# Expert stage of a four-layer kernel: products of two stages reordered and reshaped on one core

## The chip, the cores and the metric

One core of a Trainium2 chip runs the whole kernel. The metric is the device time of one execution in microseconds (us), given as the median of several runs.

## The reference

2,048 rows of 128 numbers pass four layers: a banded attention, a mixture of experts whose experts are Kronecker products, a state-space mixer with a short convolution, and a soft mixture of experts. Only the second one, cut here, is touched:

```python
def kmoe(x_flat, W_router, A, B, scale, bias, d_in1, d_in2, d_out1, d_out2, top_k):
    logits = x_flat @ W_router.T
    vals, idx = jax.lax.top_k(logits, top_k)
    probs = jax.nn.softmax(vals, axis=-1)
    xs = x_flat.reshape(-1, d_in1, d_in2)
    Y = jnp.einsum('nkoi,nij,nkpj->nkop', A[idx], xs, B[idx])
    out = jnp.einsum('nkop,nk->nop', Y, probs).reshape(-1, d_out1 * d_out2)
    return out * scale + bias
h = gelu(kmoe(x.reshape(-1, 1024), up ..., 32, 32, 64, 64, 2))
y = kmoe(h, down ..., 64, 64, 32, 32, 2)
```

There are 256 tokens of 32x32 numbers and 64 experts, of which two are taken for a token. Each of the two calls forms, for a token and an expert, A x B^T as two small products.

## The kernel before

All of this is in `kmoe` (line 648). The five engines run instruction lists of their own, written out by hand, and meet at semaphores: `wait_ge` holds back all that stands behind it on its engine. The order of the work is the order of those lists. An fp32 product appears in the trace as two matmul records with a weight load each, a transpose as one. Blocks end with a barrier of all engines, after which the next layer starts.

**Up stage.** The 256 tokens are taken in `NB` = 4 blocks `j`. `first` (L988, matmul L993) multiplies four tokens at a time, laid out block by block in `x4`, by the B tables of both experts, 16 groups `f` of four products, into banks 6 and 7 in turn. ScalarE copies each bank to `z` (`take_z`, L895, L900). `second` (L996, matmul L1007) multiplies `z` by the A tables, 128 products for a block, 32 rows by 64 columns, in two pairs, adding the two experts in PSUM. VectorE applies scale and bias (L815) into `h`, and ScalarE the gelu, two activations for a block (`gelu`, L902, L906), once the block's four parts are there. TensorE's order is first(0), first(1), second(0), first(2), second(1), first(3), second(2), second(3). ScalarE's is take_z(0), then take_z(j+1), gelu(j). The next stage (L1025) waits for all gelus. In parallel SP loads the tables of the down experts (L738 to L741), once the last up table has been gathered.

**Down stage.** The tokens are taken in `NCH` = 8 chunks. `first_down` (L1060, L1067) makes 32 products of 64 by 64 into two banks (4, 5 or 6, 7), which ScalarE copies to `vs`, one after the other (`take_v`, L922, L927). `second_down` (L1071, L1082) makes 64 products with 64 rows and 32 columns, expert by expert, adding the experts in PSUM banks 0 and 1. Chunks 2gr and 2gr+1 fill different partitions. After both, VectorE takes them out with scale and bias (`take_y`, L828, L833) into `yb`, TensorE turns them by four transposes (`rows_out`, L1086, L1093) into a bank of natural rows, and the layer norm follows: statistics and factors on VectorE (L75, L84 to L102), the root on ScalarE (L112), scaled rows on ScalarE (L933), the sum on GpSimd or VectorE (L749, L849). VectorE's list is take_y(0), then norm_y(gr), take_y(gr+1); ScalarE's is take_v(0) to take_v(5), norm_y(0), take_v(6), take_v(7), norm_y(1) to norm_y(3). TensorE's:

```python
for ch in range(NCH):
    second_down(ch)
    if ch + 2 < NCH:
        first_down(ch + 2)
    if ch >= 2 and ch % 2 == 0:
        rows_out(ch // 2 - 1)
rows_out(3)
```

The rows below also hold lines from elsewhere in this layer and the next: L958 (router logits, whose weights are read every 64 bytes of a row) and L950 (transposes of contiguous columns). L1031, L1214 and L826 are a 64-column product with a full load, a 512-column product, and a copy of one bank by VectorE.

Of the kernel before, what the change touches and what calls it, by code (L numbers as in the profile page):

```python
# [11 lines left out]
ALU = mybir.AluOpType  # L12
# [3 lines left out]
P = 128  # L16
# [631 lines left out]
def kmoe(nc, x, c, d):  # L648
# [5 lines left out]
    with ExitStack() as ctx:  # L654
# [11 lines left out]
        bias_dn = a.sb("bias_down", [P, D1])  # L666
# [14 lines left out]
        yb = a.sb("y_block", [P, 2, 8, 2, D1])  # L681
# [14 lines left out]
        y_rows = x4[:, 0:NT, :]  # L696
        oht_up = oht[:, :, :, :].rearrange("p a k (m g) -> p a k m g", m=2)
# [12 lines left out]
        v_done, v_ready, y_done, y_ready, nat_done, y_added = (a.sem(k) for k in ("v_psum", "v_ready", "y_psum", "y_ready", "y_rows_psum", "y_added"))  # L710
# [13 lines left out]
        with nc.Block() as block:  # L724
# [27 lines left out]
            def _(dve):  # L752
# [75 lines left out]
                def take_y(gr):  # L828
                    dve.wait_ge(y_done, 2 * gr + 2)
                    if gr >= 2:  # L830
                        dve.wait_ge(nat_done, gr - 1)
                    for w in range(2):
                        v.scalar_tensor_tensor(out=yb[:, gr % 2, :, w, :], in0=psum[:, w, 0:8 * D1].rearrange("p (n a) -> p n a", n=8), scalar=scales[:, 1:2],  # L833
                                               in1=bias_dn[:, :].unsqueeze(1).broadcast_to([P, 8, D1]), op0=ALU.mult, op1=ALU.add).then_inc(y_ready, 1)

                def norm_y(gr):
                    dve.wait_ge(nat_done, gr + 1)
                    for t in range(4):
                        ln_y.tile_stats(4 * gr + t, psum[:, nat_bank(gr), P * t:P * t + P])
                    ln_y.finish(dve, 4 * gr, 4 * gr + 4, gr)  # L840

                take_y(0)
                for gr in range(4):
                    norm_y(gr)
                    if gr < 3:
                        take_y(gr + 1)
# [5 lines left out]
            def _(act):  # L852
# [42 lines left out]
                def take_z(j):  # L895
                    if j >= 2:
                        act.wait_ge(h_done, 2 * j - 2)
                    for f in range(4 * j, 4 * j + 4):
                        act.wait_ge(z_done, f + 1)
                        s.copy(z[:, j % 2, 4 * (f % 4):4 * (f % 4) + 4, :, :].rearrange("p g k n -> p (g k n)"), psum[:, 6 + f % 2, :]).then_inc(z_ready, 1)  # L900

                def gelu(j):  # L902
                    act.wait_ge(hb_ready, 4 * j + 4)
                    for k in range(2):
                        part = h[:, 32 * j + 16 * k:32 * j + 16 * k + 16, :].rearrange("p n o -> p (n o)")
                        s.activation(part, part, ACT.Gelu).then_inc(gelu_done, 1)  # L906

                take_z(0)
                for j in range(NB):
                    if j + 1 < NB:  # L910
                        take_z(j + 1)
                    gelu(j)
# [9 lines left out]
                def take_v(ch):  # L922
# [3 lines left out]
                    for k in range(2):  # L926
                        s.copy(vs[:, ch % 4, k, :, :, :].rearrange("p n k b -> p (n k b)"), psum[:, v_bank(ch) + k, :]).then_inc(v_ready, 1)  # L927

                def norm_y(gr):
                    ln_y.root(act, 4 * gr, 4 * gr + 4, gr)  # L930
# [5 lines left out]
                for ch in range(6):  # L936
                    take_v(ch)
                norm_y(0)
                take_v(6)
                take_v(7)  # L940
                for gr in range(1, 4):
                    norm_y(gr)
# [976 lines left out]
```

## Time and profile before

| what | value |
|---|---|
| median of 3 runs | 874.09 us (869.92 to 874.47) |
| the profiled execution's own time | 870.78 us |
| its span | 868.8 us |
| TensorE busy | 654.9 us (75%), 7,522 matmul records |
| VectorE, ScalarE, GpSimd busy | 519.9, 344.7, 358.8 us |
| up stage | 342.0 to 390.8 us |
| down stage | 434.6 to 487.3 us |

The span is what the profiler sees between the first and last instruction; the execution's own time holds some 2 us more. In the rows below PE is TensorE's matmuls, PEld its weight loads, DVE is VectorE, ACT is ScalarE and POOL is GpSimd. "PEclk" in a window is the granted TensorE clock as a share of 2.4 GHz: 0.50 is 1.2 GHz. The time in brackets at the end of a row is how long the engine stood idle before it, and what ended that; "issue" means that nothing in the profile did.

### The profile page before, as it was taken

To read this page: it belongs to the slowest core of one execution; us is meant where nothing else is said; L and a number is where in the kernel's file an instruction comes from. 1 tells how busy PE (TensorE), PEld (TensorE's weight loads), DVE (VectorE), ACT (ScalarE), POOL (GpSimd) and SP (SyncE) were. 2 spreads that over 40 slices of the span, in tenths; PEclk is the share of its full clock that TensorE was granted. 3 is DMA by queue.
4 is the path that set the end of the run, shared out by engine and by line. 5 is a ranking of instruction groups with operands and counts; after the bars stand their busy time and mean duration, and the time that the engine had idled before them with its cause. 6 is when DMAs were issued, how large, how long until landed. Compare 5 with 4: busy or idle time off the path is not lost. (4 is left out here: it accounts for less than half of the span.)

```text
span 868.8 us, 18294 instructions
## 1 busy us (share of the span) xinstructions
PE 654.9 (75%) x7522; PEld 386.0 (44%) x7554; DVE 519.9 (60%) x1094; ACT 344.7 (40%) x522; POOL 358.8 (41%) x330
## 2 busy tenths in 40 slices
PE   0627878788786389868875478248998988999995
PEld 0313444444444389758765324123333344444442
DVE  8656666676664633221502668878999984415265
ACT  1422444334443653330423463246554535434320
POOL 9202444444442300000001062328998983966530
PEclk9968999999998579878868599659999998999999
DMA  3156540000000632200000470000000000000000
GB/s 76 36 120 150 68 66 0 0 0 0 0 1 1 223 85 49 53 3 2 2 5 5 136 235 0 0 0 1 0 1 0 0 1 1 1 0 1 12 13 24
DMA packets 17326, 29.75 MB, mean 34 GB/s; under 512 B 3248, under 2 KB 13168, under 8 KB 16240
## 3 DMA queue, kind: packets, MB, share of 16 engines
q1 hardware_dynamic: 17264, 28.87, 13.1%
q8 instruction: 46, 0.75, 0.3%
q14 instruction: 16, 0.13, 0.1%
HBM read 24.54 MB, written 4.19 MB: 33 GB/s over the span
## 5 line engine op out<-in xcount | busy, mean ns | idle before, releaser
L474 ACT ACTIVATE pr_exp<-at_psum 128x1024 f32<-128x1024 f32 x68 | 69.6, 1024 | 128.2 <-PE at_psum L559 128.2
L366 DVE TENSOR_REDUCE pr_neg_max<-at_psum 128x4 f32<-128x1024 f32 x68 | 83.2, 1225 | 49.7 <-PE at_psum L541 49.7
L316 POOL TENSOR_SCALAR_AFFINE_SELECT pr_exp<-pr_exp 128x512 f32<-128x512 f32 x68 | 47.1, 692 | 155.6 <-ACT pr_exp L474 155.6
L1481 POOL TENSOR_TENSOR all_phi_b<-all_phi_b,mo_work 128x512 f32<-128x512 f32 x56 | 71.0, 1268 | 44.6 <-ACT mo_work L1687 40.0
L749 POOL TENSOR_TENSOR all_x<-all_x,ff_x_blocks 128x512 f32<-128x512 f32 x3 | 3.8, 1267 | 187.5 <-ACT ff_x_blocks L933 187.5
L1502 PE MATMUL all_psum<-all_phi,mo_xt 128*128 128x512 f32 x128 | 66.3, 645 | 7.4 <-ACT mo_work L1669 5.6
L1451 POOL TENSOR_TENSOR mo_work<-mo_work,mo_max 128x1024 f32<-128x1024 f32 x32 | 61.4, 1918 | 21.5 <-DVE mo_max L1743 21.5
L536 PE MATMUL at_psum<-band_mask,all_ident_bf 128*128 128x512 bf16 x104 | 35.7, 401 | 40.9 <-DVE pr_q_window L359 27.6
L1535 PE MATMUL all_psum<-mo_xt,all_phi_centred 128*128 128x512 f32 x128 | 66.3, 598 | 0.0
L1588 PE MATMUL all_psum<-mo_work,mo_y_slots 128*128 128x512 f32 x128 | 62.5, 595 | 1.8 <-DVE mo_work L1791 1.8
L1687 ACT ACTIVATE mo_work<-all_psum 128x512 f32<-128x512 f32 x64 | 37.7, 601 | 61.9 <-PE all_psum L1535 61.9
L1457 POOL TENSOR_TENSOR mo_dispatch<-mo_work,mo_rsum 128x1024 f32<-128x1024 f32 x32 | 61.4, 1920 | 0.0
L1511 PE MATMUL all_psum<-mo_dispatch,mo_xn 128*128 128x512 f32 x128 | 60.1, 593 | 0.0
L1673 ACT ACTIVATE mo_work<-mo_work 128x1024 f32<-128x1024 f32 x32 | 33.9, 1059 | 55.5 <-POOL mo_work L1451 55.5
L553 PE MATMUL at_psum<-pr_neg_max_t,band_select 128*128 128x256 bf16 x272 | 41.6, 276 | 5.9 <-ACT pr_exp L474 5.5
L1791 DVE TENSOR_TENSOR mo_work<-mo_work,all_psum 128x512 f32<-128x512 f32 x64 | 38.9, 681 | 11.9 <-PE all_psum L1577 11.9
L318 POOL TENSOR_SCALAR_AFFINE_SELECT pr_exp<-pr_exp 128x512 f32<-128x512 f32 x68 | 45.8, 673 | 0.0
L1502 PEld LDWEIGHTS all_psum<-all_phi,mo_xt 128*128 128x128 f32 x128 | 23.5, 201 | 47.0 <-ACT mo_work L1669 24.8
L573 PE MATMUL at_psum<-pr_exp,pr_v_window 128*32 128x128 f32 x1088 | 41.7, 278 | 1.4 <-POOL pr_exp L318 1.4
L1743 DVE TENSOR_REDUCE mo_max<-mo_work 128x32 f32<-128x1024 f32 x32 | 38.7, 1209 | 6.5 <-ACT mo_work L1669 6.5
L1750 DVE TENSOR_REDUCE mo_sum<-mo_work 128x32 f32<-128x1024 f32 x32 | 38.7, 1209 | 0.0
L1511 PEld LDWEIGHTS all_psum<-mo_dispatch,mo_xn 128*128 128x128 f32 x128 | 24.3, 191 | 30.7 <-issue 29.6
(339 smaller groups left out, 1335.6 us busy)
## 6 DMA issues: line engine op xcount, KB each, us to landing
all_expert_w<-in_expert_w SPq DMA_DIRECT2D x1, 4096.0 KB, 18.2
ff_b_up<-in_b_up SPq DMA_DIRECT2D x1, 2048.0 KB, 9.1
ff_a_up<-in_a_up SPq DMA_DIRECT2D x1, 2048.0 KB, 14.0
ff_w_down<-in_w_down SPq DMA_DIRECT2D x2, 1024.0 KB, 20.7
at_q_stack<-parts_scratch SPq DMA_DIRECT2D x24, 64.0 KB
at_k_stack<-parts_scratch SPq DMA_DIRECT2D x24, 64.0 KB
at_q_stack<-parts_scratch SPq DMA_DIRECT2D x12, 128.0 KB
at_k_stack<-parts_scratch SPq DMA_DIRECT2D x12, 128.0 KB
```

Source lines behind the costliest of these rows:

```text
L316: nc.gpsimd.affine_select(out=e[:, g, :, 0, :], in_=e[:, g, :, 0, :], compare_op=ALU.is_ge, fill=0.0, base=0, pattern=[[0, GH], [-1, P]], ...
L318: nc.gpsimd.affine_select(out=e[:, g, :, 1, :], in_=e[:, g, :, 1, :], compare_op=ALU.is_ge, fill=0.0, base=0, pattern=[[0, GH], [1, P]], c ...
L366: nc.vector.tensor_reduce(negm[:, GH * g:GH * g + GH].rearrange("p (u r) -> p r u", r=2), psum[:, SN + 2 * (g % 2):SN + 2 * (g % 2) + 2, : ...
L474: nc.scalar.activation(e[:, g, :, :, :].rearrange("p h j q -> p (h j q)"), psum[:, ST:ST + 2, :].rearrange("p b n -> p (b n)"), ACT.Exp).t ...
L573: last = nc.tensor.matmul(psum[32 * k:32 * k + 32, PV, P * g:P * g + P], vw[:, sp, j, h, :], e[:, g, k, j, :], start=(j == 0), stop=(j == 1))
L1451: nc.gpsimd.tensor_tensor(cells(ls[:, u % 4, :]), cells(lc[:, u % 4, :]), to_cells(mn[:, u % 4, :]), ALU.subtract).then_inc(sub_done, 1)
L1457: nc.gpsimd.tensor_tensor(cells(dn[:, u % 4, :]), cells(ls[:, u % 4, :]), to_cells(rs[:, u % 4, :]), ALU.mult).then_inc(d_ready, 1)
L1481: nc.gpsimd.tensor_tensor(tot[:, ch % 2, :], first, ec[:, ch % 2, j, :], ALU.add).then_inc(added, 1)
L1502: last = nc.tensor.matmul(psum[:, 2 * hf + k, :], xt[:, P * z:P * z + P], phi_d[:, HALF * hf + W * k:HALF * hf + W * k + W], start=True, s ...
L1511: last = nc.tensor.matmul(psum[:, 4 + 2 * hf + k, :], xn[:, z, :], dn[:, u % 4, W * k:W * k + W], start=(z == 0), stop=(z == NT - 1))
L1535: nc.tensor.matmul(psum[:, n % 3, :], phi[:, P * j:P * j + P], xt[:, cols], start=False, stop=True).then_inc(cl_done, 1)
L1588: nc.tensor.matmul(psum[:, 5 + ch % 2, :], yt[:, j, :], ec[:, ch % 2, j, :], start=(j == 0), stop=(j == NJ - 1)).then_inc(y_done, 1)
```

## The change

- **Up stage, order on TensorE.** `first` now makes one group `f` and `second` a quarter of a block (one pair, half of the groups). After first(0) to first(3) each quarter of block j is followed by one group of block j+1; the last block's quarters follow each other. ScalarE's list copies two groups and then applies one gelu of a pair (one activation with 1,024 elements, strided rows), from the second pair on. The waits on banks are given by pair.
- **Down stage, shape.** `second_down` makes 32 products for a chunk instead of 64: both experts' 64 columns of `vs` by both experts' 64 columns of A. The two 32x32 blocks of the same expert in each 64x64 result are wanted, the two mixed ones are not used. Each chunk fills all of banks 0 and 1, and is taken out at once with the scale: bank 0 by ScalarE, bank 1 by VectorE.
- **Down stage, rows.** `rows_out` runs for every chunk instead of every second. Instead of a transpose it makes 8 products with 64 of the identity's columns (`pick`), which select the rows of one expert, turn them and add both in the natural bank. The bias comes first, as a product of an 8-row selector (`row_of`, a new copy on VectorE ahead of the xt copies) by the bias as 8 rows of 128.
- **Down stage, who copies.** The first of the two `vs` banks is copied by ScalarE, the second by VectorE, and the parts of the layer norm are spread in both lists. `yb` lies in a free part of `x4`.

Added lines (removed ones only where they are short; the rest of them are in the listing above):

```diff
@@ -663,7 +663,7 @@
...
-        bias_dn = a.sb("bias_down", [P, D1])
+        bias_dn = a.sb("bias_down", [R, P])
...
@@ -678,7 +678,7 @@
...
-        yb = a.sb("y_block", [P, 2, 8, 2, D1])
+        row_of = a.sb("row_of", [R, P])
...
@@ -694,6 +694,7 @@
...
+        yb = x4[:, NT:2 * NT, :].rearrange("p g n -> p (g n)").rearrange("p (u k n w a) -> p u k n w a", u=2, k=K, n=8, w=2)
...
@@ -797,6 +798,7 @@
...
+                v.tensor_copy(row_of[:, :].rearrange("r (n q) -> r n q", q=R), c["ident"][0:R, 0:R].unsqueeze(1).broadcast_to([R, 16, R])).then_inc(halves_ready, 1)
...
@@ -825,25 +827,37 @@
...
+                def take_v(ch):
+                    dve.wait_ge(v_done, ch + 1)
+                    if ch >= 4:
+                        dve.wait_ge(y_done, ch - 3)
+                    v.tensor_copy(vs[:, ch % 4, 1, :, :, :].rearrange("p n k b -> p (n k b)"), psum[:, v_bank(ch) + 1, :]).then_inc(v_dve, 1)
+
+                def take_y(ch):
+                    dve.wait_ge(y_done, ch + 1)
+                    if ch >= 2:
+                        dve.wait_ge(nat_done, ch - 1)
+                    v.tensor_scalar(yb[:, ch % 2, :, :, 1, :], psum[:, 1, :].rearrange("p (n k a) -> p k n a", n=8, k=K), scales[:, 1:2], None, ALU.mult).then_inc(y_dve, 1)
...
+                    dve.wait_ge(nat_done, 2 * gr + 2)
...
+                    ln_y.variance(dve, 4 * gr, 4 * gr + 4)
+
+                take_v(0)
+                take_v(1)
+                for ch in range(NCH):
+                    take_y(ch)
+                    if ch + 2 < NCH:
+                        take_v(ch + 2)
+                    if ch >= 3 and ch % 2 == 1:
+                        norm_y(ch // 2 - 1)
+                    if ch >= 4 and ch % 2 == 0:
+                        ln_y.invert(dve, 2 * ch - 8, 2 * ch - 4, ch // 2 - 2)
+                ln_y.invert(dve, 8, 12, 2)
+                norm_y(3)
+                ln_y.invert(dve, 12, NT, 3)
...
@@ -892,24 +906,27 @@
...
+                def take_z(f):
+                    j = f // 4
...
+                    act.wait_ge(z_done, f + 1)
+                    s.copy(z[:, j % 2, 4 * (f % 4):4 * (f % 4) + 4, :, :].rearrange("p g k n -> p (g k n)"), psum[:, 6 + f % 2, :]).then_inc(z_ready, 1)
+
+                def gelu(n):
+                    act.wait_ge(hb_ready, 2 * n + 2)
+                    rows = h[:, 32 * (n // 2):32 * (n // 2) + 32, :].rearrange("p (g r) o -> p g r o", r=4)[:, :, 2 * (n % 2):2 * (n % 2) + 2, :]
+                    s.activation(rows, rows, ACT.Gelu).then_inc(gelu_done, 1)
+
+                for f in range(4):
+                    take_z(f)
+                for n in range(2 * NB):
+                    if n < 2 * NB - 2:
+                        take_z(2 * n + 4)
+                        take_z(2 * n + 5)
+                    if n >= 1:
+                        gelu(n - 1)
+                gelu(2 * NB - 1)
...
@@ -923,23 +940,33 @@
...
+                    s.copy(vs[:, ch % 4, 0, :, :, :].rearrange("p n k b -> p (n k b)"), psum[:, v_bank(ch), :]).then_inc(v_act, 1)
+
+                def take_y(ch):
+                    act.wait_ge(y_done, ch + 1)
+                    if ch >= 2:
+                        act.wait_ge(nat_done, ch - 1)
+                    s.activation(yb[:, ch % 2, :, :, 0, :], psum[:, 0, :].rearrange("p (n k a) -> p k n a", n=8, k=K), ACT.Copy, scale=scales[:, 1:2]).then_inc(y_act, 1)
...
+                take_v(0)
+                take_v(1)
+                for ch in range(NCH):
+                    take_y(ch)
+                    if ch + 2 < NCH:
+                        take_v(ch + 2)
+                    if ch >= 3 and ch % 2 == 1:
+                        ln_y.root(act, 2 * ch - 6, 2 * ch - 2, ch // 2 - 1)
+                    if ch >= 4 and ch % 2 == 0:
+                        norm_y(ch // 2 - 2)
+                norm_y(2)
+                ln_y.root(act, 12, NT, 3)
+                norm_y(3)
...
@@ -984,38 +1011,41 @@
...
+                def first(f):
+                    if f >= 2:
+                        pe.wait_ge(z_ready, f - 1)
+                    for k in range(4):
+                        g = 4 * f + k
+                        last = t_.matmul(psum[:, 6 + f % 2, P * k:P * k + P], x4[:, g, :], gb_up[:, g, :, :].rearrange("p k n -> p (k n)"), start=True, stop=True)
+                    last.then_inc(z_done, 1)
+
+                def second(j, pair, part):
+                    q = 4 * j + 2 * pair
+                    if part == 0:
+                        pe.wait_ge(z_ready, 4 * j + 4)
+                        if q >= 6:
+                            pe.wait_ge(hb_ready, q - 4)
+                    for g2 in range(4 * part, 4 * part + 4):
+                        for k in range(K):
+                            for s in range(2):
+                                for r in (2 * pair, 2 * pair + 1):
+                                    rows = slice(32 * r, 32 * r + 32)
+                                    last = t_.matmul(psum[64 * s:64 * s + 64, h_bank(4 * j + r), F1 * g2:F1 * g2 + F1], z[rows, j % 2, 2 * g2 + s, k, :],
+                                                     ga_up[rows, 16 * j + 2 * g2 + s, k, :], start=(k == 0), stop=(k == K - 1))
+                    if part == 1:
...
+                for f in range(4):
+                    first(f)
...
+                    for pair in range(2):
+                        for part in range(2):
+                            second(j, pair, part)
+                            if j + 1 < NB:
+                                first(4 * j + 4 + 2 * pair + part)
...
@@ -1024,7 +1054,7 @@
...
-                pe.wait_ge(halves_ready, 1)
+                pe.wait_ge(halves_ready, 2)
...
@@ -1059,7 +1089,8 @@
...
+                        pe.wait_ge(v_act, ch - 1)
+                        pe.wait_ge(v_dve, ch - 1)
...
@@ -1069,28 +1100,35 @@
...
+                    pe.wait_ge(v_act, ch + 1)
+                    pe.wait_ge(v_dve, ch + 1)
+                    if ch >= 1:
+                        pe.wait_ge(y_act, ch)
+                        pe.wait_ge(y_dve, ch)
...
+                            for tl in range(2):
+                                for w in range(2):
+                                    rows, n2 = slice(64 * w, 64 * w + 64), 4 * tl + nn
+                                    last = t_.matmul(psum[64 * tl:64 * tl + 64, w, 64 * idx:64 * idx + 64], vs[rows, ch % 4, s, n2, :, :].rearrange("p k b -> p (k b)"),
+                                                     ga_dn[rows, 64 * s + 8 * ch + n2, :, :].rearrange("p k a -> p (k a)"), start=True, stop=True)
...
+                def rows_out(ch):
+                    gr = ch // 2
...
+                    pick = c["ident"][:, :].rearrange("p (c k b) -> p k c b", c=2, k=K)
+                    if ch % 2 == 0:
+                        if gr >= 2:
+                            pe.wait_ge(ln_y.by_act, 4 * (gr - 1))
+                        t_.matmul(psum[:, nat_bank(gr), :].rearrange("p (c n) -> p c n", c=4), row_of[:, :], bias_dn[:, :].unsqueeze(1).broadcast_to([R, 4, P]), start=True, stop=False)
+                    pe.wait_ge(y_act, ch + 1)
+                    pe.wait_ge(y_dve, ch + 1)
+                    for k in range(K):
+                        src = yb[:, ch % 2, k].rearrange("p n w (r q) -> p q (n w r)", q=4)
+                        for q in range(4):
+                            last = t_.matmul(out[:, q, 2 * (ch % 2):2 * (ch % 2) + 2, :], src[:, q], pick[:, k], start=False, stop=(ch % 2 == 1 and k == K - 1 and q == 3))
...
@@ -1101,9 +1139,9 @@
...
-                    if ch >= 2 and ch % 2 == 0:
-                        rows_out(ch // 2 - 1)
-                rows_out(3)
+                    if ch >= 1:
+                        rows_out(ch - 1)
+                rows_out(NCH - 1)
...
@@ -1889,7 +1927,7 @@
...
-        "bias_down": np.tile(moe["bias_down"].reshape(32, 32).T, (4, 1)),
+        "bias_down": moe["bias_down"].reshape(8, 128),
...
```

## Rows read from the trace of the kernel before

**Rows 1.** windows: us, busy (records) of PE, PEld, DVE, ACT, POOL; PEclk, DMA share, GB/s
```profile
342.00:391.00 49.00, 36.50 (x1158) 34.47 (x1160) 11.97 (x17) 18.23 (x25) 0.00 (x0) 0.83 0.20 46
442.50:455.50 13.00, 10.41 (x434) 9.15 (x432) 0.88 (x2) 3.13 (x6) 0.00 (x0) 0.50 0.02 5
434.60:487.30 52.70, 31.05 (x1552) 27.34 (x1552) 12.60 (x64) 16.61 (x37) 3.80 (x3) 0.70 0.02 4
```

**Rows 2.** timeline of TensorE, down stage: start us, us, what, [idle before <-releaser]
```profile
434.70 1.51 PE L1067 MATMUL ff_psum<-ff_b_taken,ff_h 64*64 64x64 f32 x88 [0.89 <-DVE ff_a_taken L826]
437.99 0.81 PE L1067 MATMUL ff_psum<-ff_b_taken,ff_h 64*64 64x64 f32 x40 [1.77 <-issue]
438.73 0.96 PE L1082 MATMUL ff_psum<-ff_a_taken,ff_b_up 64*32 64x32 f32 x88
441.44 0.56 PE L1082 MATMUL ff_psum<-ff_a_taken,ff_b_up 64*32 64x32 f32 x40 [1.75 <-issue]
441.93 1.67 PE L1067 MATMUL ff_psum<-ff_b_taken,ff_h 64*64 64x64 f32 x64
443.52 0.54 PE L1082 MATMUL ff_psum<-ff_a_taken,ff_b_up 64*32 64x32 f32 x24
444.89 1.61 PE L1082 MATMUL ff_psum<-ff_a_taken,ff_b_up 64*32 64x32 f32 x104 [0.83 <-issue]
...
465.70 1.98 PE L1067 MATMUL ff_psum<-ff_b_taken,ff_h 64*64 64x64 f32 x64
...
481.60 1.13 PE L1093 MATMUL ff_psum<-all_ident,ff_y_block 128*128 128x128 f32 x4 [0.99 <-DVE ff_y_block L833]
```

**Rows 3.** DMA queues, 434 to 487 us: packets, MB, share of 16 engines
```profile
q8 instruction: 13, 0.21, 1.6%
```

**Rows 4.** waits, 434 to 487 us: who waited for whom, us, times, longest
```profile
DVE ff_ln_y_tmp L100 <- ACT ff_ln_y_tmp L112: 9.3, 4, 5.2
PE ff_psum L1082 <- DVE ff_y_block L833: 6.6, 2, 4.0
```

**Rows 5.** timeline of TensorE, up stage
```profile
342.02 7.61 PE L993 MATMUL ff_psum<-ff_b_taken,ff_x_blocks 128*128 128x128 f32 x64
...
355.23 2.61 PE L1007 MATMUL ff_psum<-ff_a_taken,ff_b_up 32*64 32x64 f32 x85 [3.04 <-issue]
...
363.84 4.18 PE L1007 MATMUL ff_psum<-ff_a_taken,ff_b_up 32*64 32x64 f32 x256
...
378.87 2.06 PE L1007 MATMUL ff_psum<-ff_a_taken,ff_b_up 32*64 32x64 f32 x127 [1.29 <-issue]
382.53 3.43 PE L1007 MATMUL ff_psum<-ff_a_taken,ff_b_up 32*64 32x64 f32 x128 [1.60 <-issue]
386.26 0.92 PE L1007 MATMUL ff_psum<-ff_a_taken,ff_b_up 32*64 32x64 f32 x23 [0.30 <-issue]
```

**Rows 6.** timeline of ScalarE, up stage
```profile
345.94 0.59 ACT L900 COPY ff_b_up<-ff_psum 128x512 f32<-128x512 f32 x1 [0.31 <-PE ff_psum L993]
...
388.68 2.00 ACT L906 ACTIVATE ff_h<-ff_h 128x1024 f32<-128x1024 f32 x2 [5.73 <-DVE ff_h L815]
```

**Rows 7.** timeline and lines: prices (durations in ns as min/median/max, first and last start)
```profile
409.96 0.63 PE L1031 MATMUL ff_psum<-ff_half_sum,ff_logits_t 128*128 128x64 f32 x4 [0.48 <-DVE ff_logits_t L819]
...
357.77 3.31 PE L993 MATMUL ff_psum<-ff_b_taken,ff_x_blocks 128*128 128x128 f32 x16
...
L958 PEld LDWEIGHTS ff_psum<-ff_w_up,ff_h x32: 291/310/313, 300.2 to 306.9; 128*128 128x128 f32 x32
...
L1093 PEld LDWEIGHTS ff_psum<-all_ident,ff_y_block x16: 196/224/226, 454.4 to 482.1; 128*128 128x128 f32 x16
...
L950 PEld LDWEIGHTS ff_psum<-all_ident,ff_h x16: 183/226/231, 295.0 to 298.9; 128*128 128x128 f32 x16
...
L1214 PE MATMUL all_psum<-all_phi,sm_centre x8: 592/592/697, 542.3 to 545.4; 128*128 128x512 f32 x8
...
L826 DVE COPY ff_b_taken<-ff_psum x8: 691/692/692, 417.1 to 424.7; 128x512 f32<-128x512 f32 x8
```

More of the change, by code:

```diff
@@ L985, in _ @@
                     take_up(u)
-                def first(j):
-                    for f in range(4 * j, 4 * j + 4):
-                        if f >= 2:
-                            pe.wait_ge(z_ready, f - 1)
-                        for k in range(4):
-                            g = 4 * f + k
-                            last = t_.matmul(psum[:, 6 + f % 2, P * k:P * k + P], x4[:, g, :], gb_up[:, g, :, :].rearrange("p k n -> p (k n)"), start=True, stop=True)
-                        last.then_inc(z_done, 1)
@@ L996, in second @@
-                def second(j):
-                    pe.wait_ge(z_ready, 4 * j + 4)
-                    for r in range(4):
-                        if 4 * j + r >= 6:
-                            pe.wait_ge(hb_ready, 4 * j + r - 5)
-                    for pair in ((0, 1), (2, 3)):
-                        for g2 in range(8):
-                            for k in range(K):
-                                for s in range(2):
-                                    for r in pair:
-                                        rows = slice(32 * r, 32 * r + 32)
-                                        last = t_.matmul(psum[64 * s:64 * s + 64, h_bank(4 * j + r), F1 * g2:F1 * g2 + F1], z[rows, j % 2, 2 * g2 + s, k, :],
-                                                         ga_up[rows, 16 * j + 2 * g2 + s, k, :], start=(k == 0), stop=(k == K - 1))
+                def first(f):
[5 more added lines that the diff above has]
+                    last.then_inc(z_done, 1)
@@ L1009, in second @@
                         last.then_inc(h_done, 1)
                 pe.wait_ge(x4_part, 16)
-                first(0)
+                for f in range(4):
+                    first(f)
                 pe.wait_ge(took_act, UB)
@@ L1015, in _ @@
                 for j in range(NB):
-                    if j + 1 < NB:
-                        first(j + 1)
-                    second(j)
+                    for pair in range(2):
[3 more added lines that the diff above has]
+                                first(4 * j + 4 + 2 * pair + part)
                 pe.wait_ge(wdn_loaded, 32)
@@ L1077, in second_down @@
                             idx = 4 * (nn // 2) + 2 * s + nn % 2
-                            for k in range(K):
-                                for tl in range(2):
-                                    for w in range(2):
-                                        rows, col, n2 = slice(64 * w, 64 * w + 64), 32 * (2 * (ch % 2) + tl), 4 * tl + nn
-                                        last = t_.matmul(psum[col:col + 32, w, D1 * idx:D1 * idx + D1], vs[rows, ch % 4, s, n2, k, :],
-                                                         ga_dn[rows, 64 * s + 8 * ch + n2, k, :], start=(k == 0), stop=(k == K - 1))
+                            for tl in range(2):
[3 more added lines that the diff above has]
+                                                     ga_dn[rows, 64 * s + 8 * ch + n2, :, :].rearrange("p k a -> p (k a)"), start=True, stop=True)
```

51 lines of the change are left out of this document (1 added, 50 removed).

## The prediction

> **What bounds the kernel now.** I read the profile by stages, since the change touches two stages only. In the windows [rows 1] the up products take 342.0 to about 390.8 us with TensorE busy 36.5 of 49 us, and the down products 434.6 to 487.3 us with TensorE busy 31.1 of 52.7 us. No other engine is near full there (VectorE 12.6, ScalarE 16.6 us), so what counts is why TensorE stands still.
>
> In the timeline of the down stage [rows 2] much of the idle time is put down to "issue", nothing that the profile shows. It is regular. TensorE resumes at 437.99, 441.44 and 444.89 us, 3.45 us apart each time, and between two resumptions it runs 40+88 = 128 and then 40+64+24 = 128 matmul records. Each has its weight load, so 256 instructions. The instruction queue moved 13 packets of 16 KB in this stage [rows 3], one for about 240 of its 3,104 matmul and load instructions. I read this as instruction fetch: a block of 128 matmul records costs TensorE the larger of its work and 3.45 us. The stage's 1,552 records [rows 1] are 12.1 blocks, a floor of 41.8 us, under the 47.9 us from its first matmul to the end of its last at 482.7 us [rows 2]. The rest is waits: 6.6 us for the y evacuation L833, which stood behind the layer norm on VectorE, itself behind ScalarE's root (L100 waited 9.3 us for L112) [rows 4].
>
> The Trainium skill says otherwise (Runtime: NRT & Kernel Launch, "Instruction fetch mechanics"): crossing a 16 KiB block is mostly hidden, because the sequencer issues more slowly than the fetch fills. The blocks agree with the trace, the hiding doesn't: three resumptions come after 0.83 to 1.77 us of idle time [rows 2]. What its rule would give is a rival below.
>
> The up stage shows the same: resumptions at 382.53 and 386.26 us with 128 records between, and a longer hole of 3.04 us before 355.23 us [rows 5], when the down tables were landing (SP issues them once the last up table is gathered, near 342 us; the DMA share of this stage is 0.20, that of the down stage 0.02 [rows 1]).
>
> **The up stage.** Nothing is removed: 128 records of first and 1,024 of second. A quarter of second (64 records) costs 4.18/4 = 1.0 us and four products of first (8 records) 7.61/8 = 0.95 us, at the full clock [rows 5]. Now eight such products stand in a row and each waits for a copy out of one of two banks; after the change they lie between quarters, and the copies (0.59 us [rows 6]) lie beside second. ScalarE's gelu pair (2.00 us [rows 6]) no longer stands before the copies of the next block. New is a wait: the quarter that opens a block needs the copy of the product just before it, which I put at 0.8 us, 0.59 and a hand-over on either side.
>
> - Start: 342.0, four firsts to 345.8, wait to 346.6 us.
> - Blocks 0 to 2: 4 x 1.95 + 0.8 = 8.6 us each, above their fetch floor (288 records, 7.8 us), 25.8 us.
> - Block 3: 256 records with nothing between, two fetches, 6.9 us; the same stretch now takes 386.26 - 378.87 = 7.4 us. I take 7.2.
> - The fetch under the table loads: the records up to the hole are the same in number, but are used up earlier, at about 351.1 us. Normal supply would bring the next block right then (stall 0); the old arrival would be 355.2 us (stall 4.1). The old request waited some 1.8 us longer than usual, so I take 1.8.
>
> The sum is 346.6 + 25.8 + 7.2 + 1.8 = 381.4 us against an end of 387.2 us now: 5.8 us. The end gains more: the next stage waits for the last gelu, now two activations in 2.00 us, then one, 1.0 us less. I take 6.5 us for the stage, a little off for half clock after the stall. Bounds: 3 (stall 4.1, half clock after it) to 8.5 (no stall). VectorE's work (L815) is unchanged. Its banks' waits are not stricter.
>
> **The down stage.** Second falls from 1,024 records of 32 columns to 512 of 64 columns: the same column work, half the instructions. They have the shape of first_down: 88 records in 1.51 us, which less one pipeline length is 15 ns each [rows 2]; at half clock (the 64 records in 1.98 us) 27 ns. Now 128 records cost about 1.5 us, then 64 cost 1.0: no gain where TensorE works, only in fetch. The 16 transposes (one record each) become 64 pick products of two records: 128 records with a full 128-column load. The four records of L1031 have that load and 64 columns: 0.63 us, or 112 ns each after the first [rows 7]. At half clock the nearest is L993, 16 in 3.31 us, 207 ns [rows 7]. The bias is 4 products of 8 rows by 512 columns, 8 records, priced by L1214 at (545.4-542.3)/7 = 0.44 us [rows 7]. All in all 1,160 records, 9.1 blocks, a floor of 31.3 us.
>
> Per chunk at full clock: 1.0 + 1.0 + 16 x 0.112 + 0.44 = 4.2 us. Its 145 records have a fetch floor of 3.9 us, so TensorE becomes the bound, by a little. Step by step:
>
> - The first 128 records are first_down(0) and (1), unchanged: the resumption stays at 437.99 us.
> - The next block is 40 of first, 64 of second, 24 of first: 1.9 us of work, then 441.44 us as now.
> - The next ends with a stall to about 444.9 us. The clock of this stretch is half from 442.5 on [rows 1], as now. To the end of the first picks it then takes 1.1 (first) + 1.7 (bias) + 3.4 (picks), to about 451 us at half clock, about 450 if it rises on the way.
> - Left are 6 seconds (6.0), 4 firsts (4.0), 7 sets of picks (12.6), 3 biases (2.6): 25.2 us of full-clock work for 758 records, whose floor is 20.4 us. With 1.0 us for blocks that lie badly: 476.2 us.
>
> Now the last record ends at 482.7 us, so the stage gains 6.5 us. The waits that could stand in its way: y of a chunk is copied (0.69 us on VectorE, like L826 [rows 7], 0.59 us on ScalarE) while TensorE does first(ch+2) and picks(ch-1), 2.8 us. VectorE's norm now begins after the copies of its chunk and waits for the root a chunk later, so L833's wait is gone. Per two chunks VectorE has 4 x 0.69 plus a norm of about 2 us, under the 8.4 us of TensorE. The added v copy on VectorE spares ScalarE one of two. The y copies read twice the columns, but lie on two engines. The work after the last product stays. Bounds: gain 9.5 (full clock from the start of the stage) to a loss of 15 (below).
>
> **Small edits.** The row selector copy on VectorE stands before the xt copies: under 0.3 us. Bias rows and more wait instructions: some 0.3 us of fetch that the 1.0 covers. No DMA is added, and SP and POOL keep their order.
>
> **Sum.** -6.5 - 6.5 + 0.3 = -12.7 us against the profiled execution's 870.78 us: 858.1 us. The median of the runs, 874.09 us, lies 3.3 us above that execution, the lowest, 869.92 us, below it. I predict 860.0 us.
>
> **Rivals.**
> - *Half clock in the down stage (slower).* The picks are the dearest records at half clock. A chunk then costs 1.7 + 1.7 + 3.4 + 0.85 = 7.7 us, eight of them 61 us, an end near 498 us: 15 us lost, 6.5 gained above, 879 us. It decides in the down stage: each us at half clock does 0.55 us of work, so after the 7 us that I assume, some 28 us more at 1.2 GHz take the gain away. For it: the stage has a mean of 0.70 now [rows 1]. Against: it is idle 40% of the time now, which goes. 0.06.
> - *Strided weights (same).* The pick weights are read every 16 bytes. L958, read every 64 bytes, takes 310 ns a load and (306.9-300.2)/31 = 216 ns a record [rows 7]. If the picks did, they would cost 128 x 0.104 = 13.3 us more: 871.4 us. Against: L1093's loads, every 16 bytes, take 224 ns as L950's contiguous ones do (226) [rows 7]. 0.09. The Trainium skill (SBUF, State Buffer, "Door 1: The DMA port swizzle") has lines of 16 bytes and asks for two hits on each for full speed, which speaks for the rival; in the same note it lets four fp32 go free, which speaks for mine.
> - *The holes are not fetch (slower).* If "issue" idle time stays whatever the count, the down stage swaps work of 18 us (512 records x 15 ns, 1,024 x 8.7 by the 88 in 0.96 us, 16 x 0.11 us [rows 2]) for 33 us (8 x 4.2), less 7.6 us of waits on L833: 7.5 us longer, with 2 us won above: 876 us. That is what the Runtime page's rule would do here. The 3.45 us period speaks against it. 0.04.
> - *The tables hold the fetch (a smaller gain).* The up stage gains 3 us: 861.6 us, inside my forecast.
>
> **How the numbers follow.** My forecast has 0.78; 0.03 is for what I have not seen, 0.02 of it faster and 0.01 the same. This measurement tells about 0.5% (4.4 us) from no change: faster means under 869.7 us. Faster 0.78 + 0.02 = 0.80, same 0.09 + 0.01 = 0.10, slower 0.06 + 0.04 = 0.10. Low is 852 us (8.5 + 9.5 gained, 853, and a low run), high 871 us, which takes in the weak forms of the rivals.
>
> **What would show it.** After the change the down stage has 1,160 matmul records, picks 112 ns apart, "issue" holes only in its first 10 us, no wait for a y copy over 1 us, a clock above 0.85, and a last matmul some 34 to 42 us after its first. In the up stage no wait for z above 1 us and a stage of 41 to 46 us from its first matmul to the first of L1025's kind. Wrong would be: picks 200 ns apart at the full clock, holes that keep their sum, or a half clock past 460 us.

## The result and the profile after

The changed kernel takes 908.69 us (906.69 to 909.88, four runs) where the kernel before takes 873.13 us (869.92 to 874.47, four runs): a ratio of 1.041, 95% interval 1.038 to 1.045. It is 36 us slower; the forecast was 860.0 us in a range that ended at 871 us. The profiled execution's span is 907.2 us, against 868.8 us. Of all executions in this document two, both of `late_packed` below (873.42 and 876.38 us), lie over 1.5% above the fastest of their kernel; the ratios leave them out.

The stages, from the first matmul of the up stage to the first of the router logits, and in the down stage from its first matmul to the start of the last transpose or pick:

| kernel, profiled execution | up stage | down stage | rest of the span |
|---|---|---|---|
| before | 48.8 us | 47.6 us | 772.4 us |
| changed | 62.3 us | 66.0 us | 778.9 us |
| forecast | about 42 us | 41.5 us | unchanged |

The edits cost 13.5 and 18.4 us. 4.3 us of the rest lie before the up stage, which begins at 346.3 instead of 342.0 us. I don't charge them to the change: of the kernels below, which share that code, one begins it at 341.7 and another at 346.4 us.

These are the windows of the changed kernel, split where the clock falls; the columns are those of [rows 1]:

```profile
346.20:360.80 14.60, 10.48 (x250) 9.66 (x247) 2.10 (x3) 3.52 (x6) 0.00 (x0) 1.00 0.65 145
360.80:408.50 47.70, 42.89 (x908) 39.18 (x906) 9.86 (x14) 15.08 (x19) 0.00 (x0) 0.50 0.01 3
452.80:518.90 66.10, 61.18 (x1160) 55.42 (x1160) 17.12 (x55) 16.61 (x32) 3.80 (x3) 0.68 0.01 3
```

TensorE is hardly idle any more: it is busy 61.2 of 66.1 us in the down stage (31.1 of 52.7 in [rows 1]) and 42.9 of 47.7 us in most of the up stage. The 1,160 records are those of the forecast. The work itself has become dearer. In the up stage one row says why, the granted clock: 0.50, that is 1.2 GHz, for 47.7 us on end. Its timeline (L1033 is second, L1019 first, L1055 the logits):

```profile
353.11 1.16 PE L1033 MATMUL ff_psum<-ff_a_taken,ff_b_up 32*64 32x64 f32 x64
354.20 1.16 PE L1019 MATMUL ff_psum<-ff_b_taken,ff_x_blocks 128*128 128x128 f32 x8
355.29 1.14 PE L1033 MATMUL ff_psum<-ff_a_taken,ff_b_up 32*64 32x64 f32 x59
359.79 0.33 PE L1033 MATMUL ff_psum<-ff_a_taken,ff_b_up 32*64 32x64 f32 x5 [3.36 <-issue]
...
371.94 2.08 PE L1019 MATMUL ff_psum<-ff_b_taken,ff_x_blocks 128*128 128x128 f32 x8
373.94 1.99 PE L1033 MATMUL ff_psum<-ff_a_taken,ff_b_up 32*64 32x64 f32 x64
...
399.06 6.76 PE L1033 MATMUL ff_psum<-ff_a_taken,ff_b_up 32*64 32x64 f32 x256 [0.73 <-ACT ff_b_up L914]
408.53 18.69 PE L1055 MATMUL ff_psum<-ff_h,ff_w_down 64*64 64x128 f32 x256 [2.71 <-ACT ff_h L919]
```

At first a quarter and a group start 1.09 us apart (1.0 and 0.95 us were costed). After one hole of 3.4 us under the table loads they start 2 us apart, and the clock does not rise again before the stage is over. In the kernel before, the clock fell too (half from 353.6 to 360.4 us), but its 16 records of first in a row [rows 7] ran just there, and it was full from 360.4 to 380.9 us:

```profile
353.60:360.40 6.80, 5.17 (x97) 5.05 (x97) 1.41 (x2) 1.07 (x2) 0.00 (x0) 0.50 0.01 2
360.40:380.90 20.50, 16.59 (x671) 15.32 (x670) 5.63 (x8) 7.19 (x11) 0.00 (x0) 1.00 0.02 4
```

The down stage (L1098 is first_down, L1114 second_down, L1125 the bias, L1131 the picks), and the load of the picks:

```profile
452.86 1.51 PE L1098 MATMUL ff_psum<-ff_b_taken,ff_h 64*64 64x64 f32 x88 [0.89 <-DVE ff_a_taken L828]
456.15 0.81 PE L1098 MATMUL ff_psum<-ff_b_taken,ff_h 64*64 64x64 f32 x40 [1.77 <-issue]
456.78 1.11 PE L1114 MATMUL ff_psum<-ff_a_taken,ff_b_up 64*64 64x64 f32 x64
457.71 0.52 PE L1098 MATMUL ff_psum<-ff_b_taken,ff_h 64*64 64x64 f32 x23
459.59 0.85 PE L1098 MATMUL ff_psum<-ff_b_taken,ff_h 64*64 64x64 f32 x41 [1.36 <-issue]
460.23 1.15 PE L1114 MATMUL ff_psum<-ff_a_taken,ff_b_up 64*64 64x64 f32 x64
461.16 0.53 PE L1098 MATMUL ff_psum<-ff_b_taken,ff_h 64*64 64x64 f32 x21
463.42 0.91 PE L1098 MATMUL ff_psum<-ff_b_taken,ff_h 64*64 64x64 f32 x43 [1.73 <-issue]
464.26 1.12 PE L1125 MATMUL ff_psum<-ff_bias_down,ff_row_of 8*128 8x512 f32 x2
465.31 4.00 PE L1131 MATMUL ff_psum<-all_ident,ff_x_blocks 128*128 128x64 f32 x16
...
472.86 3.95 PE L1131 MATMUL ff_psum<-all_ident,ff_x_blocks 128*128 128x64 f32 x16
```
```profile
L1131 PEld LDWEIGHTS ff_psum<-all_ident,ff_x_blocks x128: 307/329/332, 465.3 to 518.8; 128*128 128x128 f32 x128
```

Two things are to be seen. The holes come as forecast, 3.44 and 3.83 us apart with 127 and 126 records between them, and the matmuls have none after 463.4 us, once picks lie in every block. And a set of picks takes 4.0 us instead of 1.8 or 3.4. Its records start 233 ns apart (median) at either clock, and a load takes 329 ns, like the 310 ns of L958 in [rows 7] and not like that of a contiguous one (192 ns, below). The set at 472.86 us ran almost wholly at the full clock, and the small products after it at half:

```profile
472.80:476.70 3.90, 3.90 (x24) 3.81 (x16) 0.69 (x1) 0.59 (x1) 0.00 (x0) 0.92 0.00 0
485.30:488.90 3.60, 3.60 (x129) 3.49 (x128) 0.75 (x1) 0.69 (x1) 0.00 (x0) 0.50 0.02 5
```

So the mean of 0.68 flatters the stage. From 469.2 us on the clock was full only while picks, which gain nothing from it, and a bias product ran; practically all the products of first and second ran at half.

### The profile page after: what moved, and what is told of

Read it like the earlier page. It is cut to its first block and busy times, and to the rows that moved or that the text cites. A ratio compares the mean times of both kernels' runs of the same rounds, so it can differ in the third digit from the quotient of the medians.

```text
span 907.2 us, 17592 instructions
## 1 busy us (share of the span) xinstructions
PE 712.0 (78%) x7162; PEld 431.4 (48%) x7162; DVE 527.8 (58%) x1103; ACT 347.1 (38%) x522; POOL 359.4 (40%) x330
## 5 line engine op out<-in xcount | busy, mean ns | idle before, releaser
L536 PE MATMUL at_psum<-band_mask,all_ident_bf 128*128 128x512 bf16 x136 | 43.1, 400 | 38.6 <-DVE pr_q_window L359 38.6
L1540 PE MATMUL all_psum<-all_phi,mo_xt 128*128 128x512 f32 x128 | 65.3, 636 | 7.2 <-ACT mo_work L1707 5.6
L553 PE MATMUL at_psum<-pr_neg_max_t,band_select 128*128 128x256 bf16 x272 | 41.6, 276 | 5.9 <-ACT pr_exp L474 5.5
L1540 PEld LDWEIGHTS all_psum<-all_phi,mo_xt 128*128 128x128 f32 x128 | 23.5, 198 | 44.9 <-issue 23.4
L817 DVE SCALAR_TENSOR_TENSOR ff_h<-ff_psum,ff_scales,ff_bias_up 128x512 f32<-128x512 f32 x16 | 11.3, 746 | 48.9 <-PE ff_psum L1033 48.9
```

The lines of the kernel that those rows point to most:

```text
L536: nc.tensor.matmul(psum[:, SN + 2 * (g % 2) + r, :], c["identb"][:, :], c["mask"][:, :, :].rearrange("p a b -> p (a b)"), start=True, stop ...
L1540: last = nc.tensor.matmul(psum[:, 2 * hf + k, :], xt[:, P * z:P * z + P], phi_d[:, HALF * hf + W * k:HALF * hf + W * k + W], start=True, s ...
```

## The experiments

The ratios compare each kernel with executions of the kernel before taken beside it: these have a median of 877.13 us for the first four kernels, 876.61 us for the next four (`late_packed` to `one_run`, on another chip) and 874.78 us for the last three.

**1. One edit at a time.** `down_only` is the changed kernel with the take_z, gelu, first and second code of before:

```diff
-                for j in range(NB):
-                    for pair in range(2):
-                        for part in range(2):
-                            second(j, pair, part)
-                            if j + 1 < NB:
-                                first(4 * j + 4 + 2 * pair + part)
+                for j in range(NB):
+                    if j + 1 < NB:
+                        first(j + 1)
+                    second(j)
```

> The new down stage with the old order of the up stage. Theory: the two edits lose independently; the up stage goes back to about 48.8 us from its first matmul to the first of the router logits (62.3 in the changed kernel), the down stage stays at about 71 us: 909 - 13.4 = 895 us. Rival: the up stage's loss comes from something that both edits share (place of the instructions, state of the clock before); then it stays above 55 us and the time above 902 us.

893.91 us (890.56 to 898.36), ratio 1.021 (1.017 to 1.026). The up stage is back at 48.8 us, the down stage takes 64.4 us at a clock of 0.72.

`up_only` is the reverse, the kernel before with that piece of the changed one.

> The new order of the up stage alone, with the down stage of before. Theory: the up stage takes about 62 us, with the granted clock at 0.5 from its first fetch hole to its end, and the rest is as before: 873 + 13.4 = 886.5 us. Rival: the reorder is harmless by itself (870 to 874 us).

891.35 us (887.69 to 894.27), ratio 1.016 (1.011 to 1.022). The up stage takes 63.2 us with the clock at half from 357.8 to 412.4 us, the down stage 48 us as before. So each edit loses alone, 17 and 14 us by the medians; the sum is 31 us, where both together cost 36.

**2. The pick weights.** `packed_picks` changes where the y copies put each number, so that the 128 weights of a pick are neighbours. Each copy is split in two for it:

```diff
-        yb = ....rearrange("p (u k n w a) -> p u k n w a", u=2, k=K, n=8, w=2)
+        yb = ....rearrange("p (u k q n w r) -> p u k q n w r", u=2, k=K, q=4, n=8, w=2)
...
-                        src = yb[:, ch % 2, k].rearrange("p n w (r q) -> p q (n w r)", q=4)
+                        src = yb[:, ch % 2, k].rearrange("p q n w r -> p q (n w r)")
```

> The changed kernel, with the y copies laid out so that the weights of each pick product are 128 contiguous numbers instead of every fourth one (each copy is split in two for it). Theory: the pick records took 244 ns because their weights are read every 16 bytes; contiguous they take 112 ns at the full clock or about 213 at half, so the stage gets 4 to 17 us shorter: 892 to 905 us. Rival: a load for a 64-column product that adds into a bank costs this anyway (or the bank's 32-column runs do): records stay at 244 ns, 909 us.

886.89 us (883.33 to 896.41), ratio to before 1.010 (1.005 to 1.016), where the changed kernel has 1.041. The profiled execution is the slowest of the four, so its stages are longer than those of the median. The picks of its trace, first across a rise of the clock (473.6 us), then at the full clock, last at half, and their loads:

```profile
472.61 2.44 PE L1135 MATMUL ff_psum<-all_ident,ff_x_blocks 128*128 128x64 f32 x16
...
478.05 2.00 PE L1135 MATMUL ff_psum<-all_ident,ff_x_blocks 128*128 128x64 f32 x16
...
499.80 7.09 PE L1135 MATMUL ff_psum<-all_ident,ff_x_blocks 128*128 128x64 f32 x32
```
```profile
L1135 PEld LDWEIGHTS ff_psum<-all_ident,ff_x_blocks x128: 186/270/338, 466.0 to 506.4; 128*128 128x128 f32 x128
```

A record now costs 112 ns at the full clock and 213 at half. Nothing about the product changed but the distance of its weights, so the cause of the 233 ns is shown, and the rival (the accumulation or the 32-column runs of the output) is out. The stage's first to last matmul went from 66.0 to 53.2 us.

**3. The hole under the table loads.** `late_tables` keeps the loads of the down tables back until the last up product:

```diff
                 sp.wait_ge(got, 2 * UB)
+                sp.wait_ge(h_done, 2 * NB)
```

> The changed kernel, with the loads of the down tables held back until the last product of the up stage, so that no load competes with the fetch of instructions there. Theory: the 3.4 us hole under the loads is what lets the clock fall, and the mix of quarters and groups then cannot raise it; without the hole the up stage runs at the full clock in 36 to 41 us: 884 to 889 us. Rival: the mix of small and large products lets the clock fall by itself; only the hole's 3.4 us go: about 905 us.

887.15 us (885.03 to 888.22), ratio 1.011 (1.007 to 1.016), the theory's figure. The up stage took 42.9 us, a little over the 36 to 41 expected, without a hole for 37 us and at the full clock for its first 38.9 us:

```profile
344.80:383.70 38.90, 34.06 (x1131) 31.14 (x1129) 10.56 (x15) 17.55 (x24) 0.00 (x0) 1.00 0.02 4
```

`before_late` has the same line in the kernel before:

> The kernel before with the late tables alone, the control. Theory: only the 3 us hole and the half clock behind it go, up stage 44 to 46 us, 873 to 875 us. If the late tables carry all of the gain of the kernel with the new order and late tables, this is 871 us or less, and the reorder is worth nothing.

876.12 us (870.01 to 879.01), ratio 0.998 (0.995 to 1.001): nothing. The up stage took 48.3 us, not the 44 to 46 that I expected: a hole of 1.5 us was left at the same place, the clock fell to half there all the same (358.8 to 365.6 us), and the waits for ScalarE were still there. The late loads also have a price: in every kernel that has them the time from the first router logits to the first matmul of the down stage is 45.3 to 46.9 us, where the others take 43.4 to 44.3.

**4. Both cures, and the reorder cured alone.** `late_packed` has the edits of 2 and 3, `up_late` is the kernel before with the new up order and the late tables.

> The changed kernel with both cures: tables of the down stage loaded after the up products, and contiguous pick weights. Theory: the two gains are independent and add, 22 + 22 us off 909: 865 us to, by the stages of the two profiles (19.4 + 12.8), 876 us. Rival: the second cure's gain was part of the same clock state and shrinks when the first is in: above 880 us.

> The kernel before, with the new order of the up stage and the late tables, and nothing of the new down stage. Theory: the reorder is worth what the forecast said once the clock stays at full: up stage 43 us instead of 48.8, 6 us less than before, 871 us where before has 877. Rival: same as before or slower, because the late tables delay the first down gather.

866.03 us (858.59 to 876.38, ten executions), ratio 0.987 (0.984 to 0.990), and 865.88 us (863.34 to 868.51), ratio 0.987 (0.984 to 0.991). Both beat both kernels, by 1.3% against the kernel before. The windows of `late_packed`, its up and its down stage, and rows of its timeline (L1038 second, L1024 first, L1136 picks):

```profile
346.40:387.80 41.40, 34.38 (x1155) 31.42 (x1152) 11.97 (x17) 18.60 (x25) 0.00 (x0) 0.97 0.04 10
433.10:474.50 41.40, 36.45 (x1160) 31.96 (x1160) 19.29 (x64) 19.66 (x40) 2.55 (x2) 1.00 0.02 4
```
```profile
376.60 1.16 PE L1038 MATMUL ff_psum<-ff_a_taken,ff_b_up 32*64 32x64 f32 x64
377.69 1.16 PE L1024 MATMUL ff_psum<-ff_b_taken,ff_x_blocks 128*128 128x128 f32 x8
379.58 3.52 PE L1038 MATMUL ff_psum<-ff_a_taken,ff_b_up 32*64 32x64 f32 x233 [0.73 <-ACT ff_b_up L917]
...
445.59 2.00 PE L1136 MATMUL ff_psum<-all_ident,ff_x_blocks 128*128 128x64 f32 x16
```
```profile
L1136 PEld LDWEIGHTS ff_psum<-all_ident,ff_x_blocks x128: 186/192/192, 445.6 to 474.1; 128*128 128x128 f32 x128
```

41.4 us and 41.4 us (41.0 to the start of the last pick): near the two sums of the forecast, at the full clock. The mix of quarters and groups ran at the full clock for 28 us (351.1 to 379.2) with 0.7 us waits at the block ends. In the changed kernel the rest of the mix and the last block, behind the hole, stayed at half for 47.7 us.

Against `up_late` the new down stage, even with cheap picks, shows no gain in the medians (866.03 and 865.88 us) or the ratios (0.987 both). The traces have 41.0 us for it where the old one takes 47.8 in `up_late`, but part of that is the clock, 1.00 against 0.79, and the span is only 2.3 us shorter, because the up stage began 4.8 us later (346.4 and 341.6 us). That the new shape is worth its 7 us is not shown.

**5. A dense run inside the mix.** `one_run` is the changed kernel with the four groups for the third block together, ahead of the quarters of the second:

```diff
                 for j in range(NB):
+                    if j == 1:
+                        for f in range(8, 12):
+                            first(f)
...
-                            if j + 1 < NB:
+                            if j + 1 < NB and j != 1:
```

> The changed kernel, hole and all, but with the four groups of first for the third block together again (16 records of the whole array in a row) ahead of the quarters of the second block. Theory: the clock is held at half by the mix, and a run of dense products brings it back, as in the kernel before at 360 us; from there the mix holds the full clock: up stage 48 to 54 us, 895 to 900 us. Rival: the mix falls back to half within some us whatever came before; up stage above 58 us, above 904 us.

898.46 us (894.51 to 898.54), ratio 1.025 (1.023 to 1.027). The up stage took 55.0 us, between the two.

```profile
359.43 5.07 PE L1019 MATMUL ff_psum<-ff_b_taken,ff_x_blocks 128*128 128x128 f32 x24
365.02 2.05 PE L1019 MATMUL ff_psum<-ff_b_taken,ff_x_blocks 128*128 128x128 f32 x16 [0.53 <-ACT ff_b_up L914]
367.01 4.12 PE L1033 MATMUL ff_psum<-ff_a_taken,ff_b_up 32*64 32x64 f32 x266
372.40 1.04 PE L1033 MATMUL ff_psum<-ff_a_taken,ff_b_up 32*64 32x64 f32 x54 [1.28 <-issue]
373.37 1.39 PE L1019 MATMUL ff_psum<-ff_b_taken,ff_x_blocks 128*128 128x128 f32 x8
374.69 1.99 PE L1033 MATMUL ff_psum<-ff_a_taken,ff_b_up 32*64 32x64 f32 x64
```
```profile
363.90:374.10 10.20, 8.40 (x347) 7.83 (x347) 2.82 (x4) 4.63 (x7) 0.00 (x0) 1.00 0.02 5
374.10:401.50 27.40, 23.97 (x544) 22.35 (x547) 5.64 (x8) 7.31 (x9) 0.00 (x0) 0.50 0.01 3
```

The clock came back at 363.9 us, during the run of groups. But the quarters that I had left without groups were eaten faster than the fetch supplies them, a hole of 1.3 us ended at 372.4 us, the clock fell at 374.1 with the DMA engines at a share of 0.02, and the mix stayed at half to the end. That supports the first half of the theory (a dense run raises the clock) and the two states of the mix. The time lies in the theory's range and the stage 1 us above it, but not by the theory's way, since the full clock did not last.

**6. Does the fetch floor count records?** `more_records` splits each first_down product of the kernel before into two of 32 columns.

> The kernel before, with each first_down product split into two of 32 columns: the same moving columns, 512 matmul records and their loads more, 2,064 in the stage. Theory (a block of 128 records costs at least 3.45 us): 16.1 blocks, a floor of 55.7 us; from 47.6 us the stage's first to last matmul goes to 57 to 62 us, 10 to 14 us in all. Rival (the idle time called issue does not depend on the count): only TensorE's extra work, 1 to 5 us.

892.54 us (891.78 and 893.30), ratio 1.019 (1.013 to 1.024); the stage's first to last matmul 63.3 us instead of 47.6.

```profile
442.19 4.41 PE L1069 MATMUL ff_psum<-ff_b_taken,ff_h 64*64 64x32 f32 x168 [1.96 <-issue]
446.54 0.96 PE L1083 MATMUL ff_psum<-ff_a_taken,ff_b_up 64*32 64x32 f32 x88
449.10 0.73 PE L1083 MATMUL ff_psum<-ff_a_taken,ff_b_up 64*32 64x32 f32 x40 [1.61 <-issue]
...
452.83 0.91 PE L1069 MATMUL ff_psum<-ff_b_taken,ff_h 64*64 64x32 f32 x40 [0.28 <-issue]
...
L1069 PE MATMUL ff_psum<-ff_b_taken,ff_h 64*64 64x32 f32 x1024 | 27.9, 266 | 5.6 <-issue 4.6 <-DVE ff_a_taken L826 0.9
```

It doesn't separate the two well: a record of a 64 by 64 product costs no less with 32 columns than with 64. At the full clock 88 took 1.59 us (1.51 in [rows 2]), at half 168 took 4.41 us, 26 ns each and not the 9 of second_down's 64 by 32. So TensorE's own work in first_down rose from 13.2 to 27.9 us, as much as the stage. What it does show is the pace: 256 records from 442.19 to 449.10 us, twice 3.45 us, then 128 in 3.73.

**7. The copies divided, products as before.** `spread_only` is the kernel before with the second v bank on VectorE and the parts of the layer norm spread, as in the change.

```diff
-                take_y(0)
-                for gr in range(4):
-                    norm_y(gr)
-                    if gr < 3:
-                        take_y(gr + 1)
+                for ch in range(NCH):
+                    if ch % 2 == 1:
+                        take_y(ch // 2)
+                    if ch + 2 < NCH:
+                        take_v(ch + 2)
+                    if ch >= 3 and ch % 2 == 1:
+                        norm_y(ch // 2 - 1)
...
```

> The kernel before, with its own products and transposes in both stages, and only the division of the down stage's copies taken from the change: second v bank on VectorE, root, factors and scaling spread in the lists. Theory: the waits on L833 (6.6 us) and the second v copy go, but the fetch floor of 41.8 us for 1,552 records stays: first to last matmul 42 to 45 us instead of 47.6, 3 to 6 us off: 871 to 874 us. Rival: the waits only change places (above 46 us, 876 us).

872.73 us (868.83 to 877.87), ratio 0.998 (0.995 to 1.000): at most a little. Of its waits:

```profile
PE ff_psum L1102 <- issue: 7.7, 6, 1.9
PE ff_psum L1086 <- issue: 6.8, 4, 2.3
PE ff_psum L1113 <- DVE ff_y_block L839: 1.0, 1, 1.0
```

The wait of second_down for y, 6.6 us in [rows 4], is gone, and the "issue" time rose to 14.5 us, from 9.4 in the kernel before (5.4 ahead of L1067, 4.0 ahead of L1082): first to last matmul 46.3 us, 1.3 less. The rival was right. I read it as the fetch floor taking the place of the wait, since TensorE, sooner ready, stands at the same block ends.

**8. The old products with everything that helped.** `best` has the new up order, late tables and the divided copies.

> The new order of the up stage with late tables, and the old down products with the divided copies. Theory: the two add, 866 us less 3 to 6 us: 860 to 863 us, faster than the kernel before and than every kernel so far. Rival: the down stage's gain is lost in the clock: 866 us.

865.82 us (860.34 to 870.40), ratio 0.987 (0.980 to 0.993). Up stage 40.8 us, down stage 46.2 us. Its median is that of `up_late`: the divided copies added nothing that four executions, 10 us apart, can show.

## Why the prediction was wrong

- **The bound and the fetch: right.** A block of 128 records costs at least some 3.45 us. The changed kernel shows the holes at the same spacing, and none where a block has more work than that. That these holes are instruction fetch is read from the counts of records and packets; no run shows it directly. The Trainium skill (Runtime: NRT & Kernel Launch, "Instruction fetch mechanics") calls the crossing of a block mostly hidden; here it isn't: the three holes of the changed down stage cost 4.9 us.
- **Picks at 112 ns, because 16-byte loads take as long as contiguous ones: the step that failed in the down stage.** They take 233 ns. 128 x (233-112) = 15.5 us over the full-clock price, where the rival had 13.3 us and a chance of 0.09. The row I leaned on, L1093's 224 ns against L950's 226 in [rows 7], hid the price twice. Both ran at half clock, and both were transposes, whose loads are short. My nearest price for a strided true product, L958's 216 ns, stood in the rival. In `up_late` the same strided transposes ran at the full clock, four loads in 0.56 us:

```profile
447.91 0.56 PEld L1100 LDWEIGHTS ff_psum<-all_ident,ff_y_block 128*128 128x128 f32 x4
```

  The median load of this line is 210 ns, while contiguous transposes at the full clock (L1540 in the kernel before) take 141. A strided load is some 70 ns dearer even so, and that of a true fp32 product takes 329 against 192 ns. The Trainium skill (SBUF — State Buffer, "Door 1: The DMA port swizzle") asks for two hits on a line of 16 bytes; with one number from each line the load takes 329 ns against 192, which fits, though no run here reads two. Its "4 fp32" as the stride that is free does not fit.
- **"A little off for half clock after the stall": the step that failed in the up stage.** I gave 0.3 us or so. The stage ended 20 us over my 42, 1.6 of it the longer stall and most of the rest the clock. The old order has its own repair, 16 whole-array records in a row. The new one takes that away, and its mix keeps whichever clock it finds: in the traces of `late_tables`, `late_packed`, `up_late` and `best`, with no hole ahead of it, the full one, in those of the changed kernel, `up_only` and `packed_picks` half to the stage's end. I had asked what the reorder does to waits and to the fetch, and the clock only as an average; my rival on the clock was placed in the down stage. With the loads out of the way the stage took 41.4 us in `late_packed`, 41.6 in `up_late`. That it meets my 42 is in part luck: the 42 holds 1.8 us for a stall that isn't there, and a quarter with its group takes 2.18 us, not the 1.95 costed.
- **The stall: right in place, wrong in size.** I took 1.8 us in bounds of 0 to 4.1; it was 3.36. It ended 13.5 us after the first matmul of the stage, in the kernel before 13.2: the old arrival held, and the records before it were not used up earlier, but at 10.2 us in both.
- **Waits: right.** The wait for z is 0.7 to 0.8 us a block (0.8 forecast), gelu saves its microsecond, and L833's waits are gone. But `spread_only` shows that this last one was worth almost nothing, the fetch stands behind it.
- **The down stage's clock: half right.** The mean is 0.68 at 93% busy, so "it is idle 40% of the time now, which goes" was no protection. I had put the half clock at the front, from 442.5 us for 7 us, as in the kernel before; it was full there (to 466.6 us, 13.7 us into the stage) and half for the products behind. Beside the picks the rest of the excess, 9 us, is mostly small products at 27 instead of 15 ns. And for a stage wholly at the full clock I had forecast a gain of 9.5 us, some 38 us; `late_packed`, which had that clock, took 41.0, so that this meets the forecast's 41.5 is in part luck too.

What stays open: what decides whether the down stage keeps the full clock. `late_packed` had it from end to end (1.00), `packed_picks`, with the same instructions there, a mean of 0.75; the 11 us between the lowest of `late_packed`'s executions (858.59 us at a mean clock of 0.926) and the highest that its ratio counts (869.74 us at 0.913) may be this. And `late_tables` takes away the hole and the loads at once, so that it is the hole that lets the clock fall is not shown alone. It is supported by `one_run`, where the clock fell within the first hole (353.7 us) and 1.7 us after the second, which had no loads beside it, and by `before_late`, where it fell at 358.8 us behind a hole that ended at 358.4 us, without loads. But ahead of the last two of these holes stood a long row of small products as well, and what that adds was not tested. Nor does every stop do it: the kernel before kept the full clock over a wait of 1.71 us between groups of first.

```profile
372.04 2.05 PE L993 MATMUL ff_psum<-ff_b_taken,ff_x_blocks 128*128 128x128 f32 x16 [1.71 <-ACT ff_b_up L900]
```

## What to carry to other kernels

Before an order is mixed finer, look where the granted clock recovers now and what ran there: a dense run of whole-array products may be what holds it, and a stall ahead of a thin mix can make its work take nearly twice as long. Price a strided weight load by a row of the same kind of product at the full clock; transposes at half clock hide it. Laying the copies out for contiguous weights cost little here: no product in `late_packed`'s down stage waited for them. Where instructions are fetched at a fixed pace, taking a wait away may only uncover the pace; fewer records took half of the holes away here (4.9 us of "issue" ahead of products instead of 9.4), but a gain in the whole time from that is not shown.

## What I had not expected of the hardware

- A stream of quarters and groups, with the last block behind it, ran 47.7 us on end at 1.2 GHz, 90% busy; in the kernel with no stall in front and no loads, the mix ran 28 us at 2.4 GHz.
- An fp32 load with its weights 16 bytes apart takes 329 ns and spaces the records 233 ns apart at either clock; with neighbouring weights it is 192 ns and 112 ns at the full clock, 333 ns and 213 ns at half.
- Two edits that gain nothing (late tables alone) and lose 14 us (the reorder alone) gain 11 us together.
